# Attention stage: the value products of two steps issued as one burst, with eight exponential buffers instead of four

## The chip, the cores and the metric

The kernel runs on one core of one Trainium2 chip. The metric is the device time of one execution in microseconds. Three runs of the kernel before took 1645.18, 1640.52 and 1642.26 us; the median is 1642.26 us.

## What is computed

The input is 4 batches of 1024 tokens with 256 channels. A first layer samples each token's neighbourhood, gates the result and normalises the sum with the input. A second layer (below) is pre-norm self-attention with 16 heads of 16 channels, and a mixture of 8 experts, of which each token uses the one with the largest gate. The change touches the attention's core alone.

```python
q, k, v = heads(x @ w_qkv)                       # 16 heads of 16 channels, 1024 tokens a batch
attn = jnp.einsum('bhnd,bhmd->bhnm', q, k) * (1.0 / np.sqrt(DK))
attn = jax.nn.softmax(attn, axis=-1)
y = jnp.einsum('bhnm,bhmd->bhnd', attn, v)       # the value products
x = x + y.transpose(0, 2, 1, 3).reshape(b, n, d) @ w_proj
```

## The kernel before

The program is a row of stages: sampling weights, gating and projection (`gate_and_project`), `attention`, `project_and_route`, `experts`. Each engine has its own instruction stream, written out by hand, and the streams meet at semaphores. There is no scheduler: an engine runs its instructions in the order written.

**Units and steps.** Attention runs 32 units, one for each pair of heads of one batch, and each unit has 8 steps, one for each tile of 128 keys. What one step does:

- Four score products S (L1761, into one of three PSUM banks `at_pst`): the transposed scores of 128 keys and 512 queries, for 2 heads and 2 halves of the queries. The operands are bf16 parts stacked on 96 partitions, with three more rows that subtract each query's maximum.
- Four exponentials (L1653, ScalarE, `at_pst` to `at_p`). Score product k waits until exponential k-3 has freed its bank.
- One group of value products V (L1771, float32): `values` multiplies the exponentials of a step with the values of 128 keys. It consists of four products of 32 columns by 512 queries, each into its own 32 rows of the bank `at_pacc`, which gathers the eight steps of a unit. The trace has it as 8 matmuls, 2 for each product.
- Four maximum products M (L1742, into one of three PSUM banks `at_pmx`) for a later unit, and on VectorE four reductions R (L1666) that read them. Maximum product m waits until reduction m-3 is over, since that one read its bank (`since` and `bank`).

**Order on TensorE.** `ORDER = "SSMSMVMSM"` is the order within a step. The V of step s takes the exponentials of step s-1.

**Once in a unit.** After the first step ScalarE copies the finished `at_pacc` of the unit before (L1646); in step 2, behind V, TensorE turns that copy with four transposes (`turn_out`, L1753), and VectorE forms reciprocals (L1692) and normalises (L1698) between its reductions. In step 5 (`TURN`), ahead of V, TensorE turns the maxima of the next unit (`turn_tops`, L1747); VectorE has formed them behind the last reduction of step 4 (L1671) and afterwards splits them in four small operations between reductions (L1678, L1681, L1684, L1687). SyncE's queue then writes the split rows into the operand `at_q` (L1575), and the first score product of the next unit waits for them. Units 30 and 31 have fewer or no maximum products left to make.

**Exponential buffers.** `at_p` is four tiles of two exponentials, two tiles a step. The semaphore `pv` counts V groups from `PV0 = 2`, and the exponentials of step g wait until the V group of step g-2 is done.

Of the kernel before, what the change touches and what calls it, by code (L numbers as in the profile page):

```python
# [9 lines left out]
ACT = mybir.ActivationFunctionType  # L10
AX = mybir.AxisListType
P = 128
# [5 lines left out]
BT = L // P  # L18
# [960 lines left out]
class Opening:  # L979
# [6 lines left out]
    HALF = N // 2  # L986
# [27 lines left out]
class Scores:  # L1014
# [5 lines left out]
    RING = 4  # L1020
# [477 lines left out]
def attention(nc, sem, sb, ps, io, dr, ident, w2, w_in, later, later_in, first, yn, y_out, att, pads_sent):  # L1498
# [4 lines left out]
    UNITS = B * H // 2  # L1503
    STACK, ROWS, FULL, RING, LOADS = att.STACK, att.ROWS, att.FULL, att.RING, att.LOADS
    PIECES, MAXIMA, TOPS, TURN, PER = att.PIECES, att.MAXIMA, att.TOPS, att.TURN, att.PER
    HALF = L // 2
    CHUNKS = TOKENS // HALF
    PV0 = 2
    BANKS = 3
    ORDER = "SSMSMVMSM"  # L1510

    qst, kst, vst, mx, top_, tail, top3 = att.qst, att.kst, att.vst, att.mx, att.top_, att.tail, att.top3
    ld, v_in, one_rows, red, mxmm = att.ld, att.v_in, att.one_rows, att.red, att.mxmm
    topped, topT, split, rows_in = att.topped, att.topT, att.split, att.rows_in
    pt = [sb(f"at_p{i}", [P, 2, HALF]) for i in range(4)]
    oe = sb("at_oe", [P, HALF])
    rden = sb("at_rden", [P, 8, 2])
    pst = [ps(f"at_pst{i}", [P, HALF]) for i in range(BANKS)]
# [4 lines left out]
    scored, exped, pv = (sem("at_" + n) for n in ("scored", "exp", "pv"))  # L1523
# [4 lines left out]
    with nc.Block() as block, nc.allow_non_contiguous_dma(reason="per-channel vectors"):  # L1528
        def bank(w, k):

            return (w * (4 * BT) + k) % BANKS

        def since(w, k):

            return max(0, w * (4 * BT) + k - BANKS + 1)
# [8 lines left out]
        def turns(w):  # L1544

            return w + 1 < UNITS

        def units(unit):
            for w in range(UNITS):
                unit(w, w // RING, w % RING)  # L1550

        @block.sync
        def _(sp):
# [38 lines left out]
            def unit(w, i, u):  # L1592
                first, left = w == 0, w + 3 < UNITS
                if left and not first:
                    sp.wait_ge(pv, PV0 + w * BT)
                    load(i if u == 0 else i + 1, (u + 3) % RING)
# [35 lines left out]

        @block.gpsimd
        def _(pool):
            nc.gpsimd.memset(padrow[:], 0.0).then_inc(padded, 1)
            pool.wait_ge(padded, 1)
            nc.gpsimd.iota(padrow[:, 2 * C:2 * C + 1].bitcast(I32), pattern=[[1, 1]], base=TOKENS, channel_multiplier=1,
                           allow_small_or_imprecise_dtypes=True).then_inc(padded, 1)

        @block.scalar  # L1640
        def _(a):
            def out(w):

                a.wait_ge(pv, PV0 + (w + 1) * BT)
                a.wait_ge(oT, w)
                a.copy(oe[:], pacc[:]).then_inc(oed, 1)  # L1646

            def unit(w, i, u):
                for s in range(BT):
                    for k in range(4 * s, 4 * s + 4):  # L1650
                        a.wait_ge(scored, w * (4 * BT) + k + 1)
                        a.wait_ge(pv, w * BT + s + 1)
                        a.activation(pt[k // 2 % 4][:, k % 2, :], pst[bank(w, k)][:], ACT.Exp).then_inc(exped, 1)  # L1653
                    if s == 0 and w:
                        out(w - 1)

            units(unit)
            out(UNITS - 1)
# [75 lines left out]
        @block.tensor  # L1734
        def _(pe):
            def maximum(w, u, m):
                h, nt, kh = m // (2 * BT), m // 2 % BT, m % 2
                if m == 0:
                    pe.wait_ge(ld[u], (w // RING + 1) * LOADS)
                if since(w, m):  # L1740
                    pe.wait_ge(red, since(w, m))
                nc.tensor.matmul(pmx[bank(w, m)][:], qst[u][0:ROWS, h, nt * P:(nt + 1) * P],  # L1742
                                 kst[u][0:ROWS, h, kh * HALF:(kh + 1) * HALF], start=True, stop=True).then_inc(mxmm, 1)

            def turn_tops(w):
                pe.wait_ge(topped, w + 1)
                nc.tensor.transpose(negT, top_[:], ident[:]).then_inc(topT, 1)  # L1747

            def turn_out(w):
                pe.wait_ge(oed, w + 1)  # L1750
                pmf = pm[:].rearrange("p (t x) h d -> p t (x h d)", x=2)
                for t in range(4):
                    last = nc.tensor.transpose(pmf[:, t, :], oe[:, t * P:(t + 1) * P], ident[:])  # L1753
                last.then_inc(oT, 1)

            def scores(w, u, k):

                t, p, h = k // 4, k // 2 % 2, k % 2
                if since(w, k):
                    pe.wait_ge(exped, since(w, k))  # L1760
                nc.tensor.matmul(pst[bank(w, k)][:], kst[u][:, h, t * P:(t + 1) * P],  # L1761
                                 qst[u][:, h, p * HALF:(p + 1) * HALF], start=True, stop=True).then_inc(scored, 1)

            def values(w, u, s):
                pe.wait_ge(exped, w * (4 * BT) + 4 * s + 4)
                if s == 0:
                    pe.wait_ge(oed, w)
                for p in range(2):
                    for h in range(2):
                        at = (2 * p + h) * 2 * DK  # L1770
                        last = nc.tensor.matmul(pacc[at:at + 2 * DK, :], vst[u][:, s, h, :],  # L1771
                                                pt[(2 * s + p) % 4][:, h, :], start=(s == 0), stop=(s == BT - 1))
                last.then_inc(pv, 1)

            def turn_first(t):
                if t == 0:
                    pe.wait_ge(first.y_in, 16)
                    pe.wait_ge(red, UNITS * MAXIMA)
                for k in range(KC):
                    last = nc.tensor.transpose(pY[k][:, t * P:(t + 1) * P], first.yc[:, t, k * P:(k + 1) * P], ident[:])  # L1780
                if t == first.T - 1:
                    last.then_inc(first.turned, 1)

            def project_first(t):
                if t == 0:
                    pe.wait_ge(later_in, 16 * len(later))
                    pe.wait_ge(first.yTd, 1)
                for k in range(KC):
                    last = nc.tensor.matmul(pO[t // 2][:, t % 2, :], yT[:, k, t * P:(t + 1) * P], first.wp[:, k, :],
                                            start=(k == 0), stop=(k == KC - 1))  # L1790
                if t == first.T - 1:
                    last.then_inc(first.outed, 1)

            def unit(w, i, u):
                final = w == UNITS - 1
                begun = w == 0
                pe.wait_ge(rows_in, (w + 1) * 48)
                pe.wait_ge(v_in[u], (i + 1) * 16)
                for s in range(BT):
                    ms = beside(w, u, s)  # L1800
                    k, n = 4 * s, 0
                    for what in ORDER:
                        if what == "S":
                            scores(w, u, k)
                            k += 1
                        elif what == "M":
                            if ms:
                                maximum(*ms[n])
                            n += 1
                        elif what == "V":  # L1810
                            if s == TURN and turns(w):
                                if not begun:
                                    pe.wait_ge(yd, w)
                                turn_tops(w + 1)
                            if s:
                                values(w, u, s - 1)
                            elif not begun:
                                values(w - 1, (u - 1) % RING, BT - 1)
                            if s == 2 and not begun:
                                if turns(w - 1):  # L1820
                                    pe.wait_ge(split, (w + 1) * TOPS)
                                turn_out(w - 1)
                    if final and TURNED <= s < TURNED + first.T:
                        turn_first(s - TURNED)
                    if final and s >= PROJECTED:
                        project_first(s - PROJECTED)

            TURNED, PROJECTED = 1, 6
            pe.sem_inc(pv, PV0)
            pe.wait_ge(one_rows, RING)  # L1830
            units(unit)
            project_first(BT - PROJECTED)
            values(UNITS - 1, RING - 1, BT - 1)
            project_first(BT - PROJECTED + 1)
            pe.wait_ge(yd, UNITS - 1)
            turn_out(UNITS - 1)
# [583 lines left out]
```

## Time and profile before

| | |
|---|---|
| runs, median (lowest to highest) | 1642.26 us (1640.52 to 1645.18) |
| profiled execution, first to last instruction | 1644.9 us; the profile gives no longer time for it |
| mean granted TensorE clock | 0.976 of full speed; 1.00 in attention's stretch below |
| busy in the whole span | PE 94%, DVE 81%, ACT 62%, POOL 12% |
| attention, from its first score product to its end | about 515 to 1274 us |
| one unit in the middle of it | 23.67 us (value products of one place in the unit at 897.51 and 921.18 us) |

PE is TensorE, PEld its weight loads, DVE is VectorE, ACT ScalarE, POOL GpSimd, SP and SPq SyncE and its DMA queue. Matmuls overlap: each of 512 columns is shown with 0.38 us, but the next one starts 0.22 us behind it. So starts are compared below, not durations, and a busy share of PE near 1 says only that something was always in the array.

### The profile page before, as it was taken

What the parts mean: (1) busy time and instruction counts of PE and PEld (TensorE: products, weight loads), DVE (VectorE), ACT (ScalarE), POOL (GpSimd) and SP (SyncE); (2) the same over time, 40 slices, a digit from 0 to 9 for tenths busy, and PEclk for the clock granted to TensorE, in tenths of its full rate; (3) what the DMA queues carried; (4) which work ended last, traced back from release to release, by engine and by line L of the source; (5) the groups of instructions that cost most, each with busy time, mean ns of one, the idle gap of its engine ahead of it and who ended that gap; (6) DMA issues with size and microseconds to landing.
All of it is one profiled execution on the core that took longest, in us unless ns stands there. A gap on an engine that the chain in (4) does not pass through costs nothing. (4 is left out here: it accounts for less than half of the span.)

```text
span 1644.9 us, 29425 instructions
## 1 busy us (share of the span) xinstructions
PE 1542.3 (94%) x10138; PEld 828.1 (50%) x10138; DVE 1334.3 (81%) x3019; ACT 1015.9 (62%) x1745; POOL 199.5 (12%) x372
## 2 busy tenths in 40 slices
PE   7688999979998999999999999999999869999997
PEld 7555666656653222222222222222223648999997
DVE  6899999846887889889888988888882767777773
ACT  3699998935445777777777777777777633222221
POOL 3011111131110000000000000000000451222222
PEclk9799999999998999999999999999999979999999
DMA  3300110026946222322332222223201657666661
GB/s 109 90 8 18 46 44 21 14 97 216 270 167 200 66 59 71 78 60 58 71 78 62 62 72 72 47 58 72 72 15 58 197 210 246 210 212 210 202 202 61
DMA packets 159970, 171.98 MB, mean 105 GB/s; under 512 B 73792, under 2 KB 119872, under 8 KB 159824
## 3 DMA queue, kind: packets, MB, share of 16 engines
q1 hardware_dynamic: 154416, 156.63, 32.1%
q0 software_dynamic: 4432, 13.24, 2.0%
q8 instruction: 82, 1.34, 0.3%
q14 instruction: 64, 0.52, 0.1%
q10 hardware_dynamic: 976, 0.24, 0.1%
HBM read 120.75 MB, written 49.23 MB: 103 GB/s over the span
## 5 line engine op out<-in xcount | busy, mean ns | idle before, releaser
L1666 DVE TENSOR_REDUCE at_mx<-at_pmx 128x1 f32<-128x512 f32 x980 | 617.7, 680 | 60.0 <-PE at_pmx L1742 59.1
L1653 ACT ACTIVATE at_p<-at_pst 128x512 f32<-128x512 f32 x1024 | 533.3, 605 | 212.2 <-PE at_pst L1761 212.1
L1742 PE MATMUL at_pmx<-at_k,at_q 96*128 96x512 bf16 x980 | 375.2, 383 | 0.0
L1761 PE MATMUL at_pst<-at_q,at_k 99*128 99x512 bf16 x1024 | 347.9, 381 | 4.5 <-PEq L1112 2.1
L1771 PE MATMUL at_pacc<-at_p,at_v 128*32 128x512 f32 x2048 | 273.3, 605 | 0.2 <-ACT at_oe L1646 0.2
L1742 PEld LDWEIGHTS at_pmx<-at_k,at_q 96*128 96x128 bf16 x980 | 95.4, 97 | 240.0 <-DVE at_mx L1666 180.2
L1761 PEld LDWEIGHTS at_pst<-at_q,at_k 99*128 99x128 bf16 x1024 | 99.4, 98 | 155.6 <-ACT at_p L1653 90.3
L877 PE MATMUL ws_pA<-ident,ws_A 128*128 128x128 f32 x1088 | 152.2, 287 | 24.4 <-ACT ws_A L659 22.2
L877 PEld LDWEIGHTS ws_pA<-ident,ws_A 128*128 128x128 f32 x1088 | 122.6, 146 | 84.5 <-ACT ws_A L659 37.8
L2325 DVE STREAM_TRANSPOSE ex_zr<-ex_row 32x64 f32<-32x64 f32 x608 | 143.2, 236 | 15.1 <-DMA ex_row<-scratch_routed 7.2
L2365 PE MATMUL ex_pH<-ex_zT,ex_w 128*128 128x128 f32 x1248 | 145.8, 275 | 2.2 <-ACT ex_zT L2302 2.2
L2365 PEld LDWEIGHTS ex_pH<-ex_zT,ex_w 128*128 128x128 f32 x1248 | 145.3, 192 | 4.4 <-DMA ex_w<-in_L_ffn_w 1.3
L2375 PE MATMUL ex_pY<-w,ex_hT 128*128 x624 | 141.0, 379 | 0.0
L2375 PEld LDWEIGHTS ex_pY<-w,ex_hT 128*128 128x128 f32 x624 | 115.7, 190 | 14.1
L2310 ACT ACTIVATE ex_hT<-ex_pH 128x1024 f32<-128x1024 f32 x39 | 39.9, 1022 | 121.8 <-PE ex_pH L2365 121.8
L659 ACT ACTIVATE ws_A<-ws_steps,par_beta,par_alpha 128x672 f32<-128x672 bf16 (+2 forms) x128 | 100.0, 856 | 2.8 <-issue 1.7
L659 ACT ACTIVATE ws_A<-lent_steps,par_beta,par_alpha 128x672 f32<-128x672 bf16 (+2 forms) x128 | 100.1, 854 | 1.7 <-issue 1.7
L781 DVE TENSOR_TENSOR ws_AT<-ws_pA,ws_hitT 128x768 f32<-128x768 f32 (+2 forms) x96 | 89.7, 950 | 12.4 <-PE ws_pA L877 12.2
L781 DVE TENSOR_TENSOR ws_AT<-ws_pA,lent_hits 128x768 f32<-128x768 f32 (+2 forms) x96 | 90.4, 949 | 8.5 <-PE ws_pA L877 7.9
L1942 POOL MEMSET pg_eps<- 128x1 f32 x1 | 0.1, 98 | 761.5 <-POOLq L1528 761.5
L1771 PEld LDWEIGHTS at_pacc<-at_p,at_v 128*32 128x32 f32 x2048 | 40.9, 108 | 99.0 <-ACT at_p L1653 78.9
L2302 ACT ACTIVATE ex_zT<-ex_zr,pg_lnb,pg_lnw 128x128 f32<-128x128 f32 x76 | 33.4, 486 | 73.7 <-DVE ex_zr L2325 73.7
(284 smaller groups left out, 1591.5 us busy)
## 6 DMA issues: line engine op xcount, KB each, us to landing
ex_w<-in_L_ffn_w SPq DMA_DIRECT2D x39, 1024.0 KB, 5.4
at_q<-scratch_qs SPq DMA_DIRECT2D x192, 64.0 KB, 2.8
at_k<-scratch_ks SPq DMA_DIRECT2D x192, 64.0 KB, 2.8
ex_row<-scratch_routed SPq DMA_DIRECT2D x39, 258.0 KB, 5.0
scratch_v<-gp_v SPq DMA_DIRECT2D x8, 1024.0 KB, 6.9
at_v<-scratch_v SPq DMA_DIRECT2D x32, 256.0 KB, 3.5
w<-in_L_ffn_w SPq DMA_DIRECT2D x16, 512.0 KB, 4.5
scratch_qs<-gp_split SPq DMA_DIRECT2D x16, 384.0 KB, 3.1
```

The source lines that it names most:

```text
L659: nc.scalar.activation(A[:, h % QUAD, cols(g, r)], KB[g][:, cols(g, r)], ACT.Exp, bias=par["beta"][:, t, h], scale=par["alpha"][:, t, h]). ...
L781: v.tensor_tensor(AT[h // QUAD][:, home(h, m[0]):home(h, m[-1]) + 1, :].rearrange("p s l -> p (s l)"), p[:, 0:len(m) * P], mask, ALU.mult) ...
L877: last = nc.tensor.transpose(p[:, to], a, ident[:])
L1653: a.activation(pt[k // 2 % 4][:, k % 2, :], pst[bank(w, k)][:], ACT.Exp).then_inc(exped, 1)
L1666: v.reduce_max(mx[u % 2][:, m // 2, m % 2:m % 2 + 1], pmx[bank(w, m)][:], AX.X).then_inc(red, 1)
L1742: nc.tensor.matmul(pmx[bank(w, m)][:], qst[u][0:ROWS, h, nt * P:(nt + 1) * P], kst[u][0:ROWS, h, kh * HALF:(kh + 1) * HALF], start=True, s ...
L1761: nc.tensor.matmul(pst[bank(w, k)][:], kst[u][:, h, t * P:(t + 1) * P], qst[u][:, h, p * HALF:(p + 1) * HALF], start=True, stop=True).then ...
L1771: last = nc.tensor.matmul(pacc[at:at + 2 * DK, :], vst[u][:, s, h, :], pt[(2 * s + p) % 4][:, h, :], start=(s == 0), stop=(s == BT - 1))
L2310: a.activation(hT[j % 2][:], pH[j % 2][:], ACT.Gelu_apprx_tanh).then_inc(gelu, 1)
L2325: last = v.transpose(zr[j % 2][c * Q:(c + 1) * Q, :, q * Q:(q + 1) * Q], z[q * Q:(q + 1) * Q, :, c * Q:(c + 1) * Q])
L2365: last = nc.tensor.matmul(pH[j % 2][:, c, :], w1[j % WBUFS][:, k, c * P:(c + 1) * P], zT[j % 2][:, k, :], start=(k == 0), stop=(k == KC - 1))
L2375: last = nc.tensor.matmul(pY[j % 2][:], hT[j % 2][:, c, :], w2[:, c, bass.ds(e, 1), :], start=(c == 0), stop=(c == HC - 1))
```

## The change

In every even step the V groups of the two steps before are issued one behind the other (`TOGETHER = 2`), at the place of V in that step; in an odd step nothing stands at this place. For that the exponentials have eight tiles instead of four (`PT`), and they wait for the V group of step g-4 instead of g-2 (`PV0 = 4`). At the end of the stage two V groups are issued instead of one. The four more tiles take 16 KB of each partition that the stage before still uses for tiles that go out to memory; hence two new waits for those transfers: GpSimd ahead of the fill row `padrow`, and ScalarE in unit 0 ahead of the exponentials of step 2.

```diff
-    PV0 = 2
+    PV0 = 4
     BANKS = 3
     ORDER = "SSMSMVMSM"
+    TOGETHER = 2
+    PT = 2 * PV0
...
-    pt = [sb(f"at_p{i}", [P, 2, HALF]) for i in range(4)]
+    pt = [sb(f"at_p{i}", [P, 2, HALF]) for i in range(PT)]
...
         def _(pool):
+            for done in [att.y0_out, att.v_out] + att.split_out:
+                pool.wait_ge(done, 16 * CHUNKS)
             nc.gpsimd.memset(padrow[:], 0.0).then_inc(padded, 1)
...
                 for s in range(BT):
+                    if w == 0 and s == 2:
+                        for done in [att.y0_out, att.v_out] + att.split_out:
+                            a.wait_ge(done, 16 * CHUNKS)
                     for k in range(4 * s, 4 * s + 4):
                         a.wait_ge(scored, w * (4 * BT) + k + 1)
                         a.wait_ge(pv, w * BT + s + 1)
-                        a.activation(pt[k // 2 % 4][:, k % 2, :], pst[bank(w, k)][:], ACT.Exp).then_inc(exped, 1)
+                        a.activation(pt[k // 2 % PT][:, k % 2, :], pst[bank(w, k)][:], ACT.Exp).then_inc(exped, 1)
...
-                            if s:
-                                values(w, u, s - 1)
-                            elif not begun:
-                                values(w - 1, (u - 1) % RING, BT - 1)
+                            for back in range(TOGETHER, 0, -1):
+                                if s % TOGETHER == 0 and s:
+                                    values(w, u, s - back)
+                                elif s == 0 and not begun:
+                                    values(w - 1, (u - 1) % RING, BT - back)
...
-            values(UNITS - 1, RING - 1, BT - 1)
+            for back in range(TOGETHER, 0, -1):
+                values(UNITS - 1, RING - 1, BT - back)
```

Two places in TensorE's stream show what moves. In the rows, `at_pst` is written by a score product, `at_pmx` by a maximum product, `at_pacc` by value products, `at_pm` by the transposes. The first place is the middle of unit 3, before the change: behind the V group of step 2 with its transposes, up to the V group of step 4.

```order
609 L1753 MATMUL at_pm<-ident,at_oe 128x128 x4
610 L1742 MATMUL at_pmx<-at_k,at_q 128x512
611 L1761 MATMUL at_pst<-at_q,at_k 128x512
612 L1742 MATMUL at_pmx<-at_k,at_q 128x512
613 L1761 MATMUL at_pst<-at_q,at_k 128x512 x2
614 L1742 MATMUL at_pmx<-at_k,at_q 128x512
615 L1761 MATMUL at_pst<-at_q,at_k 128x512
616 L1742 MATMUL at_pmx<-at_k,at_q 128x512
617 L1771 MATMUL at_pacc<-at_p,at_v 32x512 x4
618 L1742 MATMUL at_pmx<-at_k,at_q 128x512
```

And the same place after it, up to the burst of step 4:

```order
586 L1760 MATMUL at_pm<-ident,at_oe 128x128 x4
587 L1749 MATMUL at_pmx<-at_k,at_q 128x512
588 L1768 MATMUL at_pst<-at_q,at_k 128x512
589 L1749 MATMUL at_pmx<-at_k,at_q 128x512
590 L1768 MATMUL at_pst<-at_q,at_k 128x512 x2
591 L1749 MATMUL at_pmx<-at_k,at_q 128x512
592 L1768 MATMUL at_pst<-at_q,at_k 128x512
593 L1749 MATMUL at_pmx<-at_k,at_q 128x512 x2
594 L1768 MATMUL at_pst<-at_q,at_k 128x512
595 L1749 MATMUL at_pmx<-at_k,at_q 128x512
...
600 L1778 MATMUL at_pacc<-at_p,at_v 32x512 x8
```

Between two V places there were four score and four maximum products; now there are eight of each, and the burst behind them is twice as long. The second place is step 5 of the same unit, where the turn of the next unit's maxima stood directly ahead of a V group:

```order
631 L1761 MATMUL at_pst<-at_q,at_k 128x512
632 L1742 MATMUL at_pmx<-at_k,at_q 128x512
633 L1747 MATMUL at_pm<-ident,at_top 16x128
634 L1771 MATMUL at_pacc<-at_p,at_v 32x512 x4
635 L1742 MATMUL at_pmx<-at_k,at_q 128x512
```

After the change it stands between maximum products, in a step without V:

```order
606 L1768 MATMUL at_pst<-at_q,at_k 128x512
607 L1749 MATMUL at_pmx<-at_k,at_q 128x512
608 L1754 MATMUL at_pm<-ident,at_top 16x128
609 L1749 MATMUL at_pmx<-at_k,at_q 128x512
610 L1768 MATMUL at_pst<-at_q,at_k 128x512
```

The streams of VectorE and ScalarE keep their order and their counts.

## Rows read from the trace of the kernel before

**Rows 1.** Page: busy us of the whole span (share) and instructions of each engine.
```profile
PE 1542.3 (94%) x10138; PEld 828.1 (50%) x10138; DVE 1334.3 (81%) x3019; ACT 1015.9 (62%) x1745; POOL 199.5 (12%) x372
```
**Rows 2.** Page, costliest group of instructions: busy us, mean ns | idle before, releaser.
```profile
L1666 DVE TENSOR_REDUCE at_mx<-at_pmx 128x1 f32<-128x512 f32 x980 | 617.7, 680 | 60.0 <-PE at_pmx L1742 59.1
```
**Rows 3.** Busy PE, PEld, DVE, ACT, POOL, then clock, DMA share, GB/s, by stretch.
```profile
520.70:1228.80 708.10, 702.59 (x3971) 204.29 (x3970) 632.92 (x1164) 507.21 (x985) 0.00 (x0) 1.00 0.26 65
909.38:912.23 2.85, 2.85 (x17) 0.79 (x16) 2.46 (x6) 2.07 (x5) 0.00 (x0) 1.00 0.06 13
```
**Rows 4.** Timeline of PE, steps 4 and 5: start us, length us, instructions.
```profile
909.07 0.38 PE L1742 MATMUL at_pmx<-at_k,at_q 96*128 96x512 bf16 x1
909.38 1.06 PE L1771 MATMUL at_pacc<-at_p,at_v 128*32 128x512 f32 x8
910.38 0.39 PE L1742 MATMUL at_pmx<-at_k,at_q 96*128 96x512 bf16 x1
...
911.91 0.38 PE L1742 MATMUL at_pmx<-at_k,at_q 96*128 96x512 bf16 x1
912.65 1.06 PE L1771 MATMUL at_pacc<-at_p,at_v 128*32 128x512 f32 x8
```
**Rows 5.** The tile `at_pacc`: ns min/median/max; then PEld's timeline at a V group.
```profile
L1771 PE MATMUL at_pacc<-at_p,at_v x2048: 589/598/1063, 520.7 to 1272.6; 128*32 128x512 f32 x187
...
909.38 0.16 PEld L1771 LDWEIGHTS at_pacc<-at_p,at_v 128*32 128x32 f32 x8 [0.43 <-ACT at_p L1653]
```
**Rows 6.** Timeline of DVE in plain steps.
```profile
878.13 2.48 DVE L1666 TENSOR_REDUCE at_mx<-at_pmx 128x1 f32<-128x512 f32 x4 [0.38 <-PE at_pmx L1742]
910.81 1.29 DVE L1666 TENSOR_REDUCE at_mx<-at_pmx 128x1 f32<-128x512 f32 x2 [0.36 <-PE at_pmx L1742]
```
**Rows 7.** Timeline in the stage before, where a maximum product waits for a reduction.
```profile
438.73 0.68 DVE L1270 TENSOR_REDUCE at_mx<-gp_pM 128x1 f32<-128x512 f32 x1
439.48 0.39 PE L1442 MATMUL gp_pM<-at_k,at_q 96*128 96x512 bf16 x1 [0.57 <-DVE at_mx L1270]
```
**Rows 8.** Timeline of steps 0 to 2 of a unit: PE and ACT at the copy.
```profile
897.51 1.06 PE L1771 MATMUL at_pacc<-at_p,at_v 128*32 128x512 f32 x8
898.51 0.39 PE L1742 MATMUL at_pmx<-at_k,at_q 96*128 96x512 bf16 x1
899.15 0.60 ACT L1653 ACTIVATE at_p<-at_pst 128x512 f32<-128x512 f32 x1 [0.78 <-PE at_pst L1761]
899.65 0.58 ACT L1646 COPY at_oe<-at_pacc 128x512 f32<-128x512 f32 x1
900.11 1.60 ACT L1653 ACTIVATE at_p<-at_pst 128x512 f32<-128x512 f32 x3
```
**Rows 9.** Timeline of step 2: the transposes, the reciprocals and the normalisation.
```profile
903.22 1.06 PE L1771 MATMUL at_pacc<-at_p,at_v 128*32 128x512 f32 x8
904.21 0.66 PE L1753 MATMUL at_pm<-ident,at_oe 128*128 128x128 f32 x4
904.70 0.38 PE L1742 MATMUL at_pmx<-at_k,at_q 96*128 96x512 bf16 x1
905.73 0.41 DVE L1698 TENSOR_TENSOR at_yn<-at_pm,at_rden 128x256 f32<-128x256 f32 x1
906.06 4.39 DVE L1666 TENSOR_REDUCE at_mx<-at_pmx 128x1 f32<-128x512 f32 x7
```
**Rows 10.** Timeline of DVE at the tops, and of SPq and PE behind the split.
```profile
887.75 0.68 DVE L1666 TENSOR_REDUCE at_mx<-at_pmx 128x1 f32<-128x512 f32 x1
888.55 1.28 DVE L1666 TENSOR_REDUCE at_mx<-at_pmx 128x1 f32<-128x512 f32 x2
892.55 0.27 DVE L1687 TENSOR_TENSOR at_top<-at_tail,at_top 16x128 bf16<-16x128 f32 x1
892.85 1.78 SPq L1575 DMA_DIRECT2D at_q<-at_top  x3
896.33 0.60 PE L1761 MATMUL at_pst<-at_q,at_k 99*128 99x512 bf16 x2
```

More of the change, by code:

```diff
@@ L1771, in values @@
                         last = nc.tensor.matmul(pacc[at:at + 2 * DK, :], vst[u][:, s, h, :],
-                                                pt[(2 * s + p) % 4][:, h, :], start=(s == 0), stop=(s == BT - 1))
+                                                pt[(2 * s + p) % PT][:, h, :], start=(s == 0), stop=(s == BT - 1))
                 last.then_inc(pv, 1)
```

## Prediction

> **What bounds the kernel now.** I read the page first, then the groups, then attention by stretches, then single steps on a timeline.
>
> The page says that PE is busy 94% of the span and DVE 81% [rows 1]. That names no bound, because PE's matmuls overlap. The groups say where the time goes: the 980 reductions of attention take 617.7 us of DVE, 680 ns each, and DVE stood idle for 59 us ahead of them, waiting for the maximum products [rows 2]. The reader is to see that DVE is starved a little, regularly. By stretches, PE is in use for 702.6 of 708.1 us of attention and DVE for 632.9, with TensorE's clock granted in full (1.00, the 2.4 GHz level); in one plain step of 2.85 us DVE works 2.46 [rows 3].
>
> The timeline says why. From one V group to the next, TensorE starts something every 0.22 us: the next M follows the V group by 1.00 (909.38 to 910.38), seven more starts come at (911.91 - 910.38)/7 = 0.219, and the next V group follows the last M by 0.31 (909.07 to 909.38) [rows 4]. That sums to 1.00 + 7 x 0.219 + 0.31 = 2.84, the whole step, so nothing in a plain step waits: TensorE sets the pace. DVE starts a reduction 0.43 behind its product (910.38 to 910.81), then one every (2.48 - 0.68)/3 = 0.60, and pauses 0.36 to 0.38 once in a step, across the V group [rows 4, 6]. So two engines are close together: TensorE needs 2.84 for a step, DVE 4 x 0.60 = 2.40 and small operations. The chain of waits follows only the end of the program and says nothing on attention.
>
> **What the change takes from TensorE.** A V group costs 1.00 + 0.31 where an ordinary start costs 0.22, so 1.09 more. Its eight matmuls last 1.06 together and one lasts 0.598 [rows 4, 5], so the second half starts 0.46 after the first. Two halves more in the same burst should cost 0.92, and a double burst 1.92 instead of 1.00. A pair of plain steps then costs TensorE 1.92 + 15 x 0.219 + 0.31 = 5.51 instead of 5.68: 0.17 less, in 4 pairs of 32 units 22 us. That is all the change can give, and it holds only if the eight M of a pair can be issued at 0.22 spacing.
>
> The unknown here is the second group. At the low end it costs as much as the length of one product, 0.60; near it, four starts of 0.219, 0.88. At the high end it costs what a group costs now, 1.09. I take 0.92, since the weight loads of the second half of a group, all eight in 0.16 us, are already issued while the first half runs [rows 5].
>
> **What it does to DVE.** The order of DVE's work is untouched, but its supply is not. There are three banks, and product m waits for reduction m-3. Call R0 to R7 the reductions of the eight M that follow a double burst. M7, the last before the next burst, waits for R4. Nothing of the burst may start before M7, because TensorE runs in order. So a new chain closes, and its length is the least time of a pair, counted from the first M behind a burst:
> - M0 to the start of R0: 0.43 [rows 4, 6]
> - R0 to the start of R4, four spacings of 0.60: 2.40 [rows 6]
> - R4 itself: 0.68 [rows 6, 10]
> - end of R4 to start of M7: 0.07. Before, this wait occurs in attention never, but in the stage ahead of it: a reduction ends at 439.41 and the product starts at 439.48 [rows 7]
> - M7 to the burst: 0.31; the burst to the next M0: 1.92.
>
> The sum is 5.81, against TensorE's own 5.51 and today's 5.68. In today's single steps the same chain is 0.43 + 0.68 + 0.07 + 0.31 + 1.00 = 2.49, since M3 waits for R0 only; it is hidden under 2.84. That is the difference between the two orders: three banks hold some 1.9 us of work for DVE, enough for a burst of 1.00 with its approach, not for 1.92. So a plain pair is 0.13 longer, not 0.17 shorter. ScalarE's chain is nearly the same: its first exponential starts 0.64 behind M0, the spacing is (1.60 - 0.60)/2 = 0.50, and the eighth score product waits for the fifth exponential, 0.64 + 2.00 + 0.60 + 0.07 = 3.31, M7 0.22 later at 3.53, beside DVE's 3.58 [rows 8].
>
> **The four pairs of a unit.** What stands between reductions or exponentials is now on these chains, where it was hidden before:
> - Steps 0 to 2 (V of step 0 at 897.51, of step 2 at 903.22, 5.71): the copy of `at_pacc` comes behind the first exponential. 0.64 + 0.50 + 0.46 (copy, 899.65 to 900.11) + 3 x 0.50 + 0.60 + 0.07 + 0.22 + 0.31 + 1.92 = 6.22, so +0.51 [rows 8, 9].
> - Steps 2 to 4 (903.22 to 909.38, 6.16): the four transposes take 0.49 behind the burst (904.21 to 904.70), the normalisation delays R1 by 0.33 (905.73 to 906.06). 5.81 + 0.82 = 6.63, +0.47 [rows 4, 9].
> - Steps 4 to 6 (3.27 from 909.38 to 912.65, and 2.84, so 6.11): the top maxima put 888.55 - 887.75 - 0.60 = 0.20 between two reductions, and the first split about the same (estimated from its likes of 0.27, of which part overlaps). 5.81 + 0.40 = 6.21, +0.10 [rows 4, 10]. The turn of the maxima stops waiting ahead of a V group and stands among the M, where it is covered.
> - Steps 6 to 0: 5.81 against 5.68, +0.13.
>
> A unit grows by 1.21 us. Thirty units have all their maximum products: 36 us. Unit 30 has the first two pairs (+1.0). Behind them only the exponentials close a chain, 0.42 + 2.00 + 0.60 + 0.07 + 0.31 + 1.92 = 5.32 for a pair against 4.80, partly covered by other work: about 1 for five pairs. The stage's end has a burst of two groups instead of one: 0.9. Together +39; I take +38, since half-covered waits were all counted full.
>
> **Edits that cost nothing.** The wider wait of the exponentials (g-4) is met long before. ScalarE comes to its new wait two steps into unit 0, some 5.7 us (2 x 2.84) after the stage before ended; if the last transfers are late, that is a few us once, which the range holds. GpSimd's fill row is needed in unit 2 only. The rows split from the maxima go out nearly as before: issued from 892.85, three in 1.78, while the next unit's first score starts at 896.33, 3.51 after the split ended at 892.82 [rows 10]. In the new order DVE ends the split later against that start. Behind the burst of step 4, R4 starts at 0.43 + 2.40 + 0.40 = 3.23, and two reductions and the other splits later (1.20 + 0.20 + 0.14 + 0.60) the last split starts at 5.37 and ends at 5.64. The burst of step 6 starts at 3.23 + 0.68 + 0.07 + 0.31 = 4.29, ends at 6.21, and the unit's first score is the twelfth start behind it, 11 x 0.219 = 2.4 and some 0.2 of waiting for banks: 8.8. So they are 3.2 apart. If all of today's 3.51 were needed, that is 0.3 in 30 units, 9 us; I take none, and the upper end keeps it.
>
> The sum was made inside one profiled execution of span 1644.9; the median of the runs is 1642.26, and +38 puts the forecast at 1680.
>
> **Rivals.**
> 1. *TensorE alone decides, faster.* If DVE and ScalarE do not hold back the eighth products, the pair falls to 5.51 and the kernel to 1642 - 22 = 1620. For it: PE has no idle time in the plain step and both others have. Against it: the bank counting, in which M7 waits for R4 whatever TensorE saves. Beside it stands a rule of the Trainium skill, TensorEngine Tiling (Array Packing), Key Properties: changing the tiling mode drains the engine, tiles of one mode do not. By that rule merging removes one drain in two, which is this rival's gain; the rows agree that entry and exit cost time (1.31 for a group against 0.92 for its halves), but they do not bound the pair by it.
> 2. *The second group pays the full price, slower still.* If it costs 1.09, every pair grows by a further 0.17: 22 us, 1702. Against it: the early weight loads. The Trainium skill, TensorE: Matmul & The Clock Gate, The mechanism, states that weight loads overlap running matmuls only where the row groups differ; here all rows are used by all, so by that rule the second group's loads would wait and this rival would hold. The trace does not agree within a group.
> 3. *No change.* Then the burst has to be 0.30 cheaper, 1.62, the second group costing 0.62, about one product's length: 1642. Nothing speaks for that but the overlap of the four column groups.
> 4. *The chains hold in part.* Release and spacing could be shorter in a fuller pipeline; 0.07 less in 4 pairs and 32 units is 9 us, and half the growth is 1660.
>
> **How the numbers follow.** Forecast (1668 to 1694 as its own range): 0.72. Rival 2: 0.09. Rival 4: 0.06. Rival 3: 0.06. Rival 1: 0.07. The range 1656 to 1700 leaves out rivals 1 and 3 and about half of rival 2, some 0.18. A measurement of this kernel tells 0.3%, 5 us, from no change. Faster 0.07, same 0.06, slower 0.87.
>
> **What would show it.** In the profile after: V bursts of 16 matmuls lasting about 1.98, the next M 1.92 behind their start. One idle stretch of DVE per pair near 1 us or more, instead of two of 0.36. Maximum and score products with real waits for reductions and exponentials ahead of each burst. Units 24.9 apart instead of 23.67. Everything outside attention unchanged. I am wrong if the M ahead of a burst starts without waiting for R4, or if units come closer than 23.67.

## The result, and the profile after

| | before | after |
|---|---|---|
| median (lowest to highest) | 1643.72 us (1640.52 to 1648.52), 4 runs | 1672.93 us (1671.45 to 1675.77), 4 runs |
| ratio, 95% interval | | 1.0188 (1.0163 to 1.0213) |
| profiled execution, span | 1644.9 | 1670.1 |
| attention, start of the first score product to start of the last transpose | 759.4 | 787.1 |
| all the rest of the span | 885.5 | 883.0 |

The median of the kernel before has one run more here than in the section on its time, 1648.52 us. The medians lie 29 us apart. Between the two profiled executions the span grew by 25.2 us: attention by 27.7, while all the rest together was 2.5 shorter. So the loss lies in attention.

The page of the kernel after, its share of busy time and its two costliest groups, which answer to [rows 1, 2] (behind the new lines the line numbers are higher, in these rows by 7):

```profile
PE 1552.1 (93%) x10138; PEld 841.8 (50%) x10138; DVE 1325.8 (79%) x3019; ACT 1012.0 (61%) x1745; POOL 198.6 (12%) x372
...
L1660 ACT ACTIVATE at_p<-at_pst 128x512 f32<-128x512 f32 x1024 | 529.5, 617 | 243.3 <-PE at_pst L1768 238.8
L1673 DVE TENSOR_REDUCE at_mx<-at_pmx 128x1 f32<-128x512 f32 x980 | 611.5, 681 | 66.9 <-PE at_pmx L1749 66.9
```

Nothing in this page would show a loss at first sight. Every count is the same, and a reduction lasts as long as before. The idle time that waits for TensorE's products grew from 59.1 to 66.9 us on DVE, far less than the loss, and from 212.1 to 238.8 on ScalarE, nearly as much; it comes in small pieces over the whole stage.

The stretches say more. Columns as in [rows 3]: four pairs of steps of one unit, each from the start of one burst to the next (0 to 2, 2 to 4, 4 to 6, 6 to 0).

```profile
882.99:889.13 6.14, 5.93 (x34) 1.66 (x33) 5.27 (x10) 4.42 (x10) 0.00 (x0) 1.00 0.24 74
889.13:895.68 6.55, 6.36 (x37) 2.12 (x36) 5.03 (x10) 4.40 (x9) 0.00 (x0) 1.00 0.74 174
895.68:901.82 6.14, 5.88 (x34) 1.79 (x33) 5.24 (x12) 4.24 (x10) 0.00 (x0) 1.00 0.00 0
901.82:907.57 5.75, 5.75 (x34) 1.71 (x33) 5.42 (x11) 3.85 (x9) 0.00 (x0) 1.00 0.01 2
```

They sum to 24.58 us, a unit; before it was 23.67. The clock is full in all of them. In three of the four PE now has gaps (5.93 of 6.14 us in use in the first); before it had one only in the pair with the turn of the maxima (5.95 of 6.11). In the fourth, the plain pair, the overlap of the matmuls covers the waits, and only the starts show them. (Before, every step had its V group: the rows of the first place under The change run up to that of step 3, not of step 4.)

The plain pair in detail, the timeline of PE, then of DVE and of ScalarE, which answers to [rows 4, 6]:

```profile
903.68 0.39 PE L1749 MATMUL at_pmx<-at_k,at_q 96*128 96x512 bf16 x1
...
905.68 0.38 PE L1768 MATMUL at_pst<-at_q,at_k 99*128 99x512 bf16 x1
906.05 0.39 PE L1749 MATMUL at_pmx<-at_k,at_q 96*128 96x512 bf16 x1
906.28 0.60 PE L1768 MATMUL at_pst<-at_q,at_k 99*128 99x512 bf16 x2
...
906.93 0.39 PE L1768 MATMUL at_pst<-at_q,at_k 99*128 99x512 bf16 x1
907.25 0.39 PE L1749 MATMUL at_pmx<-at_k,at_q 96*128 96x512 bf16 x1
907.57 1.92 PE L1778 MATMUL at_pacc<-at_p,at_v 128*32 128x512 f32 x16
909.42 0.39 PE L1749 MATMUL at_pmx<-at_k,at_q 96*128 96x512 bf16 x1
```

```profile
904.11 4.88 DVE L1673 TENSOR_REDUCE at_mx<-at_pmx 128x1 f32<-128x512 f32 x8 [0.34 <-PE at_pmx L1749]
909.85 0.69 DVE L1673 TENSOR_REDUCE at_mx<-at_pmx 128x1 f32<-128x512 f32 x1 [0.87 <-PE at_pmx L1749]
```

```profile
904.32 4.03 ACT L1660 ACTIVATE at_p<-at_pst 128x512 f32<-128x512 f32 x8 [1.91 <-PE at_pst L1768]
```

Read the chain from these rows, with the names of the prediction: M0 to M7 are the eight maximum products behind a burst, R0 to R7 their reductions. M0 starts at 903.68 and R0 at 904.11, 0.43 later. Eight reductions follow without a gap, spaced (4.88 - 0.68)/7 = 0.60; R4, the fifth, starts at 906.51 and ends at 907.19. M7 starts at 907.25, 0.06 behind it. The burst follows by 0.32, lasts 1.85 to the next M at 909.42, and the next reduction starts at 909.85. DVE stood idle for 0.87. The product at 906.05 stands 0.37 behind the start ahead of it instead of 0.22: that is M5, with the same kind of wait, for R2.

ScalarE's chain is close behind. Its exponentials are spaced (4.03 - 0.60)/7 = 0.49, so the fifth ends at 904.32 + 4 x 0.49 + 0.60 = 906.88, and the eighth score product, which needs its bank, starts at 906.93. From there M7 could have started 0.22 later, at 907.15. DVE's chain ends last, but by 0.10 only.

### The profile page after: what moved, and what is told of

Read it like the earlier page. It is cut to its first block and busy times, and to the rows that moved or that the text cites. A ratio compares the mean times of both kernels' runs of the same rounds, so it can differ in the third digit from the quotient of the medians.

```text
span 1670.1 us, 29431 instructions
## 1 busy us (share of the span) xinstructions
PE 1552.1 (93%) x10138; PEld 841.8 (50%) x10138; DVE 1325.8 (79%) x3019; ACT 1012.0 (61%) x1745; POOL 198.6 (12%) x372
## 5 line engine op out<-in xcount | busy, mean ns | idle before, releaser
L1660 ACT ACTIVATE at_p<-at_pst 128x512 f32<-128x512 f32 x1024 | 529.5, 617 | 243.3 <-PE at_pst L1768 238.8
L1673 DVE TENSOR_REDUCE at_mx<-at_pmx 128x1 f32<-128x512 f32 x980 | 611.5, 681 | 66.9 <-PE at_pmx L1749 66.9
L1749 PE MATMUL at_pmx<-at_k,at_q 96*128 96x512 bf16 x980 | 367.5, 384 | 8.7 <-DVE at_mx L1673 5.7
L1768 PE MATMUL at_pst<-at_q,at_k 99*128 99x512 bf16 x1024 | 354.9, 382 | 12.0 <-PEq L1112 2.1
L1778 PE MATMUL at_pacc<-at_p,at_v 128*32 128x512 f32 x2048 | 246.2, 598 | 0.0
L1778 PEld LDWEIGHTS at_pacc<-at_p,at_v 128*32 128x32 f32 x2048 | 53.4, 109 | 112.3 <-ACT at_p L1660 65.1
```

The lines of the kernel that those rows point to most:

```text
L1660: a.activation(pt[k // 2 % PT][:, k % 2, :], pst[bank(w, k)][:], ACT.Exp).then_inc(exped, 1)
L1673: v.reduce_max(mx[u % 2][:, m // 2, m % 2:m % 2 + 1], pmx[bank(w, m)][:], AX.X).then_inc(red, 1)
```

## Experiments

**Buffers and waits without the grouping.**

```diff
-    TOGETHER = 2
+    TOGETHER = 1
```

> The eight exponential buffers, the wider wait (g-4) and both new waits for the earlier transfers, but one V group in every step as before (TOGETHER = 1). Theory (bank chain: with a double burst the last maximum product before it waits for a reduction three places back): buffers and waits cost nothing, so the time of the kernel before, 1643 us within 3, and units 23.67 us apart. Rival (placement of the tiles or the new waits cost the time): some or all of the +29 us, up to 1673.

Measured: 1638.2 us against 1639.8 of the kernel before on the same chip, ratio 0.9992 (0.9976 to 1.0007). Its plain steps are 2.84 us apart. So eight tiles, their place in memory, the wait g-4 and both new waits cost nothing that these runs can tell (1 us at most by the interval), and the loss belongs to the order on TensorE.

**Four groups in one burst.** Ten tiles suffice, if they are used in one running order over all units.

```diff
-    PV0 = 4
+    PV0 = 5
-    TOGETHER = 2
+    TOGETHER = 4
-    a.activation(pt[k // 2 % PT][:, k % 2, :], pst[bank(w, k)][:], ACT.Exp).then_inc(exped, 1)
+    a.activation(pt[(w * 2 * BT + k // 2) % PT][:, k % 2, :], pst[bank(w, k)][:], ACT.Exp).then_inc(exped, 1)
...
-    pt[(2 * s + p) % PT][:, h, :], start=(s == 0), stop=(s == BT - 1))
+    pt[(w * 2 * BT + 2 * s + p) % PT][:, h, :], start=(s == 0), stop=(s == BT - 1))
```

> Four V groups in one burst in every fourth step, ten exponential tiles in one running order (PV0 = 5). Theory (bank chain): three banks hold DVE for the same time whatever the burst's length, so each added group of 0.86 us is added to DVE's pause. The burst grows from 1.85 to 3.56 us, per four steps TensorE saves about 0.2 more, and DVE pauses once for about 2.6 instead of twice for 0.87: units near 26.2 instead of 24.59, time 1673 + 49 = 1722 (1712 to 1732). Rival (the loss comes from something that a burst pays once, entry, exit or the first waits behind it): half as many bursts, half of the loss, 1658.

Measured: 1714.1 us, ratio 1.0447 (1.0427 to 1.0468), which is 74 us over the kernel before, 43 over two groups (1.0188 of the same 1639.8 is 1670.7); 49 were expected. The timeline of PE and of DVE around one burst:

```profile
888.38 3.64 PE L1778 MATMUL at_pacc<-at_p,at_v 128*32 128x512 f32 x32
...
891.95 0.39 PE L1749 MATMUL at_pmx<-at_k,at_q 96*128 96x512 bf16 x1
```

```profile
892.38 1.29 DVE L1673 TENSOR_REDUCE at_mx<-at_pmx 128x1 f32<-128x512 f32 x2 [2.58 <-PE at_pmx L1749]
```

The burst takes 888.38 to 891.95, 3.57, and DVE waits 2.58 in one piece, 1.71 more than at a double burst for 1.72 more of burst. Each group added is added to the pause in full. Half as many bursts did not halve the loss; the rival fell.

The other burst of the same unit shows a second cost. PE and then DVE:

```profile
900.59 0.60 PE L1768 MATMUL at_pst<-at_q,at_k 99*128 99x512 bf16 x2 [0.17 <-DMA at_q<-at_top]
```

```profile
905.78 0.69 DVE L1673 TENSOR_REDUCE at_mx<-at_pmx 128x1 f32<-128x512 f32 x1 [2.82 <-PE at_pmx L1749]
```

Here the first score product of the next unit waits for the split rows, which SyncE's queue writes into `at_q`. It starts 3.01 behind the end of the last split (897.58), and the pause is 2.82 instead of 2.58. In 31 units the 0.24 is 7 us of the 43 (an estimate from this one unit; the trace has such waits 31 times). So with four groups the order on TensorE begins to cost through this wait too.

**A small copy.**

```diff
-    a.copy(oe[:], pacc[:]).then_inc(oed, 1)
+    n = HALF if w == 0 else 32
+    a.copy(oe[:, 0:n], pacc[:, 0:n]).then_inc(oed, 1)
```

> The changed kernel, but from unit 1 on ScalarE copies only 32 of the 512 columns of at_pacc (the other columns of the copy stay as unit 0 left them, so the attention's result is left incomplete). Theory: in the pair of steps 0 to 2 the exponentials close the chain and the copy of 0.46 us stands in it; without most of it this pair falls from 6.14 to about 5.8 and the others stay: 0.3 us in 32 units, 10 us, so 1663 (1660 to 1666). Rival (the copy is beside the path, and the pair is long for another reason): no change, 1673.

Measured: 1657.9 us, ratio 1.0107 (1.0085 to 1.0128), so 13 us below two groups with the whole copy (1670.7) where 10 were expected; the time itself is below the stated 1660 to 1666, as the kernel before, too, takes 4 us less here than in the first comparison. The four pairs are 5.74, 6.56, 6.14 and 5.74 us in the order of the stretches above: the pair with the copy fell from 6.14 to the plain pair's length, 0.40 less and in 32 units 13 us, and the others are the same. ScalarE's timeline shows how little stands between the first exponential and the next seven:

```profile
883.38 0.60 ACT L1661 ACTIVATE at_p<-at_pst 128x512 f32<-128x512 f32 x1 [1.72 <-PE at_pst L1769]
883.87 0.18 ACT L1651 COPY at_oe<-at_pacc 128x32 f32<-128x32 f32 x1
883.94 3.56 ACT L1661 ACTIVATE at_p<-at_pst 128x512 f32<-128x512 f32 x7
```

The second exponential follows the copy's start by 0.07; in the changed kernel it is 0.47 (885.98 to 886.45).

**The turn behind the group, in the kernel before.** Here the single groups stay; only the turn of the next unit's maxima moves.

```diff
 elif what == "V":
-    if s == TURN and turns(w):
-        if not begun:
-            pe.wait_ge(yd, w)
-        turn_tops(w + 1)
...
+    if s == TURN and turns(w):
+        if not begun:
+            pe.wait_ge(yd, w)
+        turn_tops(w + 1)
```

> The kernel before, one group in every step, with the turn of the next unit's maxima in step 5 issued behind the V group instead of ahead of it. In the kernel before TensorE waits there for the top maxima: from the last maximum product to the V group 0.74 us instead of 0.31. Theory: behind the group the maxima are long ready, and the turn costs about 0.2 us of TensorE, so 0.2 to 0.3 us in 31 units are won: 7 us, 1636 (1634 to 1639). Rival (DVE, whose first split now comes later, becomes late and gives it back): 1643.

Measured: 1628.5 us against 1639.8, ratio 0.9928 (0.9912 to 0.9944): 11 to 12 us faster than the kernel before, and faster than everything else here that computes the whole result. Below is TensorE's timeline in step 5, first a row of the kernel before that [rows 4] leave out, then this run:

```profile
912.45 0.27 PE L1747 MATMUL at_pm<-ident,at_top 128*16 128x128 f32 x1 [0.16 <-DVE at_top L1671]
```

```profile
903.28 0.38 PE L1742 MATMUL at_pmx<-at_k,at_q 96*128 96x512 bf16 x1
903.59 1.06 PE L1771 MATMUL at_pacc<-at_p,at_v 128*32 128x512 f32 x8
904.59 0.28 PE L1747 MATMUL at_pm<-ident,at_top 128*16 128x128 f32 x1
904.70 0.38 PE L1742 MATMUL at_pmx<-at_k,at_q 96*128 96x512 bf16 x1
```

Compare [rows 4]: there 0.74 us lay between the last M (911.91) and the V group (912.65), because the turn waited for the top maxima until 912.45 and then took 0.20. Now it is 0.31, and behind the group the turn takes 0.11. The long step, from V group to V group, is 2.95 instead of 3.27. 0.32 in 31 units is 10 us; I had expected 7, since I had set the turn at 0.2. DVE's first split comes 0.11 later (4.15 behind the V group of the step before instead of 4.04) and gives nothing back.

**Halved reductions, one group and two.** Both kernels, each with this edit, which leaves out half of each maximum:

```diff
-    v.reduce_max(mx[u % 2][:, m // 2, m % 2:m % 2 + 1], pmx[bank(w, m)][:], AX.X).then_inc(red, 1)
+    v.reduce_max(mx[u % 2][:, m // 2, m % 2:m % 2 + 1], pmx[bank(w, m)][:, 0:HALF // 2], AX.X).then_inc(red, 1)
```

> The kernel before with every reduction of the attention stage over 256 of its 512 columns (half of each maximum is left out). It is the partner of the next run. A reduction should then last about 0.42 us, spaced 0.34 instead of 0.60 (estimate). Theory (in single steps TensorE sets the pace, DVE is hidden): plain steps stay at 2.84; only the wait for the top maxima in step 5 shrinks, 0.27 us a unit, 1640 - 8 = 1632. Rival (DVE sets the pace here already): steps fall well below 2.84.

> The changed kernel with the same halved reductions. Theory: DVE's chain for a pair (0.43 + 4 spacings + 0.68 + 0.07 + 0.31 + 1.85) loses 4 x 0.26 + 0.26 = 1.3 us and is no longer last; the chain of the exponentials, 0.64 + 2.0 + 0.6 + 0.07 + 0.22 + 0.31 + 1.85 = 5.6 to 5.7, takes its place, and in steps 0 to 2 with the copy 6.14 stays. So plain pairs fall only from 5.74 to about 5.6, steps 2 to 4 from 6.56 to about 6.1, 4 to 6 from 6.14 to about 5.7; units 23.6, 1671 - 32 = 1639. Rival (the burst itself costs TensorE more than it saves): nothing changes, units 24.6, 1671.

Measured, one group: 1627.6 us against 1639.2 of the kernel before on this chip, ratio 0.9925 (0.9907 to 0.9944). All plain steps are still 2.84 us, and the step of the turn falls from 3.27 to 2.95. Two groups: 1636.2, ratio 0.9984 (0.9967 to 1.0001). The pairs, in the order 0 to 2, 2 to 4, 4 to 6, 6 to 0, are 6.14, 6.13, 5.65, 5.65. So with less work for DVE the grouped kernel gains 34 us (1.0188 of 1639.2 is 1670.0; 32 were expected) and the single one 12 (8 were expected). It stops where ScalarE's chain was expected: the pair with the copy did not move at all, and the plain pair fell only by the 0.10 that lie between the two chains. ScalarE's timeline and then PE's, two groups:

```profile
882.05 4.03 ACT L1660 ACTIVATE at_p<-at_pst 128x512 f32<-128x512 f32 x8 [1.62 <-PE at_pst L1768]
```

```profile
884.66 0.39 PE L1768 MATMUL at_pst<-at_q,at_k 99*128 99x512 bf16 x1
884.89 0.38 PE L1749 MATMUL at_pmx<-at_k,at_q 96*128 96x512 bf16 x1
885.20 1.92 PE L1778 MATMUL at_pacc<-at_p,at_v 128*32 128x512 f32 x16
```

The fifth exponential ends at 882.05 + 4 x 0.49 + 0.60 = 884.61; the eighth score product, M7 and the burst follow without another wait. With DVE out of the way the grouping still costs 9 us (1636.2 against 1627.6).

**Both halved, one group and two.** The edit above, and this one, which from unit 1 on leaves out half of the exponentials too (in the kernel before with `% 4` in place of `% PT`):

```diff
-    a.activation(pt[k // 2 % PT][:, k % 2, :], pst[bank(w, k)][:], ACT.Exp).then_inc(exped, 1)
+    n = HALF if w == 0 else HALF // 2
+    a.activation(pt[k // 2 % PT][:, k % 2, 0:n], pst[bank(w, k)][:, 0:n], ACT.Exp).then_inc(exped, 1)
```

> The kernel before with halved reductions and, from unit 1 on, exponentials over 256 of 512 columns (half of each maximum and half of the exponentials are left out). Theory: TensorE alone was the pace and stays it, 2.84 for a plain step; 1632 or a few us less, since the last two units have no cover: 1625 to 1632. Rival: plain steps below 2.84.

> The changed kernel with both halved in the same way. Theory: both chains are off the path, and TensorE alone sets the pace: a plain pair 1.85 + 15 x 0.219 + 0.31 = 5.44 instead of 5.68 for two single steps, so units near 22.4, and this run is faster than its partner with one group in a step by 0.24 x 4 x 32 = 30 us, give or take 6: about 1600. That would be the gain the grouping has when nothing else holds it. Rival (a double burst gives TensorE nothing): equal to its partner, 1625 to 1632.

Measured, one group: 1627.6 us, ratio 0.9917 (0.9902 to 0.9931), plain steps 2.84. Two groups: 1599.3, ratio 0.9764 (0.9701 to 0.9828), pairs of 5.44, 5.92, 5.56 and 5.44. Here the grouping wins 28 us over its partner, where 30 were expected (two runs of the one, six of the other; their times do not overlap). PE's timeline, two groups:

```profile
884.98 0.38 PE L1750 MATMUL at_pmx<-at_k,at_q 96*128 96x512 bf16 x1
885.20 0.38 PE L1769 MATMUL at_pst<-at_q,at_k 99*128 99x512 bf16 x1
885.41 0.59 PE L1750 MATMUL at_pmx<-at_k,at_q 96*128 96x512 bf16 x2
885.85 0.38 PE L1769 MATMUL at_pst<-at_q,at_k 99*128 99x512 bf16 x1
...
887.15 0.38 PE L1750 MATMUL at_pmx<-at_k,at_q 96*128 96x512 bf16 x1
887.46 1.92 PE L1779 MATMUL at_pacc<-at_p,at_v 128*32 128x512 f32 x16
889.32 0.39 PE L1750 MATMUL at_pmx<-at_k,at_q 96*128 96x512 bf16 x1
```

No start waits now: (887.15 - 884.98)/10 = 0.217 for ten starts, the burst 0.31 behind the last one, and 1.86 from the burst to the next M. The gain of the double burst on TensorE is real, 0.24 us a pair. What takes it away in the whole kernel are the waits for the two readers.

**Two banks instead of three for the maximum products,** one group and two:

```diff
+    def bank_m(w, m):
+        return (w * (4 * BT) + m) % 2
...
-    pe.wait_ge(red, since(w, m))
+    pe.wait_ge(red, w * MAXIMA + m - 1)
```

The maximum products and their reductions then take the bank from `bank_m`.

> The kernel before, but the maximum products of the attention stage rotate over two of the three banks, so product m waits for reduction m-2. Theory: the chain of a single step becomes 0.43 + 0.60 + 0.68 + 0.07 + 0.31 + 1.00 = 3.09 and is now last in place of TensorE's 2.84; with the small operations units near 25.9 instead of 23.67, so 1640 + 70 = 1710 (1700 to 1722). Rival (bank counts do not matter while DVE keeps up on average): 1640.

> The changed kernel with two banks for the maximum products. Theory: the product ahead of a burst now waits for reduction R5 instead of R4, one spacing of 0.60 more in each pair, a plain pair 5.74 + 0.6 = 6.34; steps 0 to 2, which the exponentials close at 6.14, rise only to 6.34 as well. Units 24.6 + 3 x 0.6 + 0.2 to 0.4 = 26.7, so 1670 + 68 = 1738 (1725 to 1750). The loss by grouping is then 0.16 in a plain pair (6.34 against 2 x 3.09). Rival: 1670.

Measured, one group: 1712.6 us against 1645.7 of the kernel before on this chip, ratio 1.0408 (1.0378 to 1.0438), plain steps 3.09 us apart, which is the chain's sum to the hundredth. Two groups: 1740.3, ratio 1.0576 (1.0546 to 1.0607), plain pairs 6.34 (891.59 to 897.93 in this timeline of PE), again the sum. Both times lie in the expected ranges.

```profile
891.59 1.92 PE L1782 MATMUL at_pacc<-at_p,at_v 128*32 128x512 f32 x16
893.45 0.39 PE L1753 MATMUL at_pmx<-at_k,at_q 96*128 96x512 bf16 x1
...
897.61 0.39 PE L1753 MATMUL at_pmx<-at_k,at_q 96*128 96x512 bf16 x1
897.93 1.92 PE L1782 MATMUL at_pacc<-at_p,at_v 128*32 128x512 f32 x16
```

Nothing but a bank was taken away, and both orders pay what the chain says. In the single order it has to grow past 2.84 first (from 2.49 to 3.09 is +0.60, of which 0.25 is seen). The opposite, a fourth bank for the maxima, was not tried: all eight banks are in use (three, three, `at_pacc`, `at_pm`).

## Why the prediction was right, step by step

- **What bounds the kernel before.** TensorE, with DVE hidden under it. Shown: with halved reductions, and with both halved, plain steps stay at 2.84.
- **What the burst saves.** Predicted 0.17 a pair, measured 0.24 where nothing holds it back (5.44 against 5.68).
- **The chain over the three banks.** Predicted 5.81 for the plain pair, measured 5.75. Its parts, predicted and measured: 0.43 and 0.43; four spacings of 0.60 and 0.60; 0.68 and 0.68; release 0.07 and 0.06; approach 0.31 and 0.32; burst 1.92 and 1.85. With two banks and with four groups the chain moved by the amount that it gives; with halved reductions it fell away, and ScalarE's chain, predicted 0.05 shorter and measured 0.10 shorter, took its place at 5.65.
- **The burst was priced too high.** This is the term that was off. I took the second half of a group 0.46 behind the first, from the union of its eight matmuls less the length of one; over two groups the measured cost of the second is 0.85 to 0.86, not 0.92. 0.07 in 4 pairs and 32 units is 9 us. Of the values that I weighed (0.60, 0.88, 0.92, 1.09) four starts of 0.219, 0.88, was nearest.
- **The pairs of a unit.** Predicted growth 0.51, 0.47, 0.10, 0.13; measured 0.43 (6.14 from 5.71), 0.39 (6.55 from 6.16), 0.03 (6.14 from 6.11), 0.07 (5.75 from 5.68). Each is 0.06 to 0.08 lower, and the burst's 0.07 covers that to 0.01. The copy's place in the first pair is shown by the small copy.
- **The ends of the stage, and the sum.** Unit 0 was 2.2 us shorter, which was not foreseen (last section); units 30 and 31 cost 3.6 us more than before, where 3 were put. So attention grew by 29 units of 0.91 (26.4) less 2.2 plus 3.6, 27.7 us, where 39 had been added up and 38 taken. Most of the distance is the burst's price; the 3.4 us of unit 0 (2.2 shorter instead of 1.2 longer) are chance in these two executions.
- **The turn of the maxima.** I wrote that among the M it would be covered. It is not waited for by the path, but TensorE does wait there: the product ahead of it starts at 899.07 and the turn at 899.61. DVE's chain hides that. In the kernel before the same wait was on the path. The forecast counts it, in the step of 3.27, but passes over that it can be removed by itself: moving the turn gave 11 to 12 us (1639.8 to 1628.5) without any grouping.
- **Edits at nothing.** Shown by the run with buffers and waits alone. The rows split from the maxima are in time with two groups. The end of the split and the start of the next unit's first score product:

```profile
902.90 0.27 DVE L1694 TENSOR_TENSOR at_top<-at_tail,at_top 16x128 bf16<-16x128 f32 x1
```

It ends at 903.17, and that product starts at 906.28 (in the rows of the plain pair), 0.23 behind the M ahead of it and so without a wait; 3.2 were predicted and 3.11 are there. The margin is thin: in the run with four groups, at 3.01, the product waited.
- **The rivals.** The gain on TensorE alone (1620) exists, at 1599 against 1628, once both readers are fast. The full price of the second group is refuted by the burst of 1.85. The Trainium skill, TensorE: Matmul & The Clock Gate, The mechanism, says in one place that weight loads overlap running matmuls only where the row groups differ; by that the second group would have paid it, and the trace does not agree (in the burst that runs from 882.99 to 884.91 the second group's loads are shown at 883.44 and 883.87, see the rows below). The same section also lets a load go ahead if it goes into the background weight buffer, and that the trace does not contradict. The Trainium skill, TensorEngine Tiling (Array Packing), Key Properties, says that changing the tiling mode drains the engine; the saving of 0.24 us a pair on TensorE is in line with it, but no run here tells a drain from another cost of beginning and ending a burst.

```profile
883.44 0.13 PEld L1778 LDWEIGHTS at_pacc<-at_p,at_v 128*32 128x32 f32 x4 [0.30 <-ACT at_p L1660]
883.87 0.13 PEld L1778 LDWEIGHTS at_pacc<-at_p,at_v 128*32 128x32 f32 x4 [0.30 <-issue]
```

## What to carry to other kernels

Before work on an engine is gathered into a longer burst, count what its readers hold in their buffers: with n banks the last item issued ahead of the burst waits for the reader's item n places back, and from there on the whole burst and its approach lie on the path. Average idle time of the reader (here 0.36 us a step) does not protect it; the number of banks times the reader's time per item does. Do this for every reader: here ScalarE's chain was only 0.10 shorter than DVE's, and making DVE alone faster did not make the burst pay. And when the engine itself sets the pace, look first for the one place in a period where its spacing is broken by a wait, since moving that single instruction behind the next independent work may be enough: here it gave 11 to 12 us, where the regrouping lost 29.

## What the runs showed that was not expected

- Four float32 products of 32 columns by 512, side by side, cost TensorE 0.86 us when they follow others of their kind (3.57 us for four groups: 0.86 for each beyond the first), and 1.00 when they end a burst, with 0.31 ahead of the burst where an ordinary start takes 0.22.
- A float32 transpose of 16 columns by 128 costs 0.11 us of TensorE directly behind such a burst (904.59 to 904.70), and 0.20 ahead of one (912.45 to 912.65 in the kernel before).
- Unit 0 began at a low granted clock in both kernels, and left it at different times. Below is the stretch of four us that begins 2.9 us behind the first score product, before and then after (columns as in [rows 3]; the last but two is the clock). Before, the starts were still 0.43 apart, the 1.2 GHz level, when the first V group came at 520.70, and the next M followed it by 1.50 instead of 1.00; after, the spacing had fallen from 0.43 to 0.22 at 517.5, the 2.4 GHz level, and the first burst at 520.67 took 1.85. The order did not decide it. In the six profiles with single groups the last slow product (over 0.5 us long instead of 0.38) starts 2.9 to 5.2 us behind the first score product; in the six with bursts it is 2.9 to 8.1. So the 2 us of unit 0 are put down to chance.

```profile
518.00:522.00 4.00, 4.00 (x15) 0.96 (x13) 2.74 (x5) 2.28 (x4) 0.00 (x0) 0.53 0.57 132
```

```profile
517.00:521.00 4.00, 4.00 (x19) 1.45 (x21) 4.00 (x8) 3.63 (x8) 0.39 (x2) 0.92 0.54 131
```
